# Planning the first eight expert tiles early and running the end of the first attention among them

## What is computed

```python
h = _L0_tok_ref(x, L0_tok_W, L0_tok_b)             # moving averages, then a projection
h = h + _L0_attn_ref(_layernorm(h, axis=-1), ...)  # causal softmax attention, 16 heads
h = h + _L0_ffn_ref(_layernorm(h, axis=-1), ...)   # 8 experts, 256 -> 1024 -> 256, top 2 a token
h = h + _L1_attn_ref(h, ...)                       # sigmoid(s) * exp(s) attention
h = h + _L1_ffn_ref(_layernorm(h, axis=-1), ...)   # fp8 product
```

## Time and profile before

| | us |
|---|---|
| median of 3 runs | 851.28 (846.99 to 853.36) |
| the profiled execution | 855.8 |
| its span, first to last instruction | 854.0 |
| TensorE busy | 730.1 (85%), mean granted clock 0.911 |
| first attention | to about 264 |
| tiles, from the first second layer | 308.9 to 591.4 |
| second attention | 591 to about 817 |
| fp8 layer | to 854 |

### The profile page before, as it was taken

One profiled execution on the slowest core, in us unless ns is written; L12 is line 12 of the kernel. 1 busy time (PEld: TensorE's weight loads), 2 busy tenths in 40 slices (PEclk: granted clock), 3 DMA queues, 4 the chain that ended last, 5 costly groups with the idle time before them and its releaser, 6 DMA issues. The chain is left out here.

```text
span 854.0 us, 15973 instructions
## 1 busy us (share of the span) xinstructions
PE 730.1 (85%) x5604; PEld 580.3 (68%) x5604; DVE 447.0 (52%) x1111; ACT 349.9 (41%) x596; POOL 121.7 (14%) x166
## 2 busy tenths in 40 slices
PE   6488989889886299999999999998589888898646
PEld 5367767767664199999999999997366555664312
DVE  4536776776465222333223132231667888766677
ACT  3143345325432022222222132223687888988513
POOL 2010131232123300000010000101332223100000
PEclk9799999999999599999999999999798988998855
DMA  7989366346541555555565559740764466642002
GB/s 178 206 127 211 45 84 81 64 65 87 72 114 52 177 206 198 179 181 172 173 202 185 182 152 230 218 173 31 112 90 65 66 79 100 74 54 23 1 13 86
DMA packets 70710, 102.66 MB, mean 120 GB/s; under 512 B 8160, under 2 KB 58472, under 8 KB 70512
## 3 DMA queue, kind: packets, MB, share of 16 engines
q1 hardware_dynamic: 66928, 92.82, 49.0%
q0 software_dynamic: 3136, 8.40, 3.3%
q10 hardware_dynamic: 576, 0.52, 0.2%
HBM read 63.88 MB, written 12.58 MB: 90 GB/s over the span
## 5 line engine op out<-in xcount | busy, mean ns | idle before, releaser
L1623 PEld LDWEIGHTS psum<-arena 128*128 128x128 f32 x1248 | 147.1, 194 | 3.5 <-issue 1.7
L1623 PE MATMUL psum<-arena 128*128 128x128 f32 x1248 | 147.7, 277 | 1.1 <-ACT arena L1254 1.1
L1657 PE MATMUL psum<-arena 128*128 x624 | 141.3, 379 | 1.2 <-DVE arena L1458 1.2
L1657 PEld LDWEIGHTS psum<-arena 128*128 128x128 f32 x624 | 115.5, 190 | 15.7 <-issue 1.6
L1248 ACT ACTIVATE arena<-psum,arena 128x128 f32<-128x128 f32 x156 | 44.5, 368 | 197.4 <-PE psum L1623 140.3
L1585 PE MATMUL psum<-arena 96*128 96x256 bf16 x512 | 84.4, 299 | 26.3 <-ACT arena L1219 15.1
L1451 DVE TENSOR_SCALAR arena<-psum,arena 128x128 f32<-128x128 f32 x156 | 43.9, 344 | 94.7 <-PE psum L1623 75.2
L1585 PEld LDWEIGHTS psum<-arena 96*128 96x128 bf16 x512 | 47.1, 103 | 62.3 <-ACT arena L1219 26.9
L1343 DVE TENSOR_TENSOR arena<-arena 128x1024 f32<-128x1024 f32 x64 | 80.0, 1314 | 5.5 <-ACT arena L1218 3.1
L1219 ACT ACTIVATE arena<-psum,neg_mu 128x1024 f32<-128x1024 f32 x64 | 68.9, 1118 | 13.8 <-PE psum L1585 8.2
L1188 POOL DMA_INDIRECT w0T<-yg,pos x32 | 31.1, 971 | 301.0 <-DMA yg<-arena 239.3
(11 more groups left out here) (248 smaller groups left out, 1157.9 us busy)
## 6 DMA issues: line engine op xcount, KB each, us to landing
arena<-in_L_ffn_w_dram SPq DMA_DIRECT2D x47, 1024.0 KB, 5.4
arena<-arena SPq DMA_DIRECT2D x192, 128.0 KB, 6.0
arena<-xg SPq DMA_DIRECT2D x39, 128.0 KB, 2.0
yg<-arena SPq DMA_DIRECT2D x39, 128.0 KB, 1.7
out_dram<-arena SPq DMA_DIRECT2D x8, 256.0 KB, 2.1
arena<-in_x_dram SPq DMA_DIRECT2D x8, 128.0 KB, 7.3
arena<-in_L_ffn_b_dram SPq DMA_DIRECT2D x1, 1024.0 KB, 12.2
xg<-zeros SPq DMA_DIRECT2D x5, 128.0 KB
```

Source lines behind the costliest of these rows:

```text
L1623: mm = pe.matmul(psum[:, 2 * v + c // HALF, (c % HALF) * P:(c % HALF + 1) * P], w1b[:, i % W1_BUFS, d, c * P:(c + 1) * P], xtT[:, v, d, :] ...
L1657: mm = pe.matmul(y_bank, hidT[:, u, c, :], w2s[:, one(e), c, :].rearrange("p o n -> p (o n)"), start=(c == 0), stop=(c == HC - 1))
```

## The change

Blocks 1 and 2 become one. All engines but GpSimd stop `batches` after iteration 7. What iterations 8 and 9 did is written out as `drain_...` pieces and set among the steps of the first tiles, from step -2 to step 3.

The list of tiles is made in two parts. From the counts after five batches (`EARLY_BATCHES`) DVE picks tiles that are full already (`early_valid` at the end of iteration 6, `early_grid` and `early_list` in iteration 7, with two products of TensorE each), and lists the first eight. SP loads the weights and rows of tile 0 as soon as that list is there and the rows of five batches have landed. The rest of the list (`late_valid`, `late_grid`, `late_list`) is made in steps 3 and 4; from tile 8 on SP waits for it, for all scatters, and for the zero rows, which SP now writes alone, all eight in its step 4.

A tile list in two parts makes the slots harder to find: 22 small DVE steps in place of ten, in steps 11 to 14. `gather(0)` waits for 24 tiles in place of 16, and so everything for the first batch stands seven steps later; `combine(1)`, `stat1(1)` and `norm1(1)` stand two later, in steps 36, 37 and 38. Some banks of PSUM change places. Iteration 0 to 5 of the first attention, the work of a tile, the second attention and the fp8 layer are as before.

```diff
+EARLY_TILES, EARLY_BATCHES = 8, 5
...
-        def batches(eng, iteration):
+        def batches(eng, iteration, end):
 
             for b in range(-2, 2):
                 iteration(b, b % 2, b // 2)
             with eng.Fori(0, (B - 4) // 2) as it:
                 for u in range(2):
                     iteration(it * 2 + (2 + u), u, it + 1)
-            for b in range(B - 2, B + 2):
+            for b in range(B - 2, end):
                 iteration(b, b % 2, b // 2)
...
-                batches(sp, iteration)
-
+                batches(sp, iteration, B)
...
                 load_w2(7)
-                zero_tails(sp, range(0, EXPERTS, 2))
-                sp.wait_ge(S["p_step"], TILE_E_STEP)
+                sp.wait_ge(S["st_mm"], PAIRS * (B - 1))
+                sp.wait_ge(S["p_step"], EARLY_STEPS)
                 load_w1(sp, 0)
-                sp.wait_ge(S["zfill"], 16 * (EXPERTS + 1))
                 for u in range(2):
-                    sp.wait_ge(scat[u], 16 + 16 * TOPK * QT * B // 2)
-                sp.wait_ge(S["p_step"], PLAN_STEPS)
+                    sp.wait_ge(scat[u], 16 + 16 * TOPK * QT * ((EARLY_BATCHES + 1 - u) // 2))
                 load_tile(sp, 0)
-
+                sp.wait_ge(S["st_mm"], PAIRS * B)
+
...
+                def tile(i, u):
+                    if i == 2:
+                        sp.dma_start(w8, a["L1_ffn_weight"].rearrange("(j p) i -> p j i", p=P)).then_inc(S["w8_in"], 16)
+                    if i + 3 == EARLY_TILES:
+                        sp.wait_ge(S["p_step"], PLAN_STEPS)
+                        sp.wait_ge(S["zfill"], 16 * (EXPERTS + 1))
+                        for s in range(2):
+                            sp.wait_ge(scat[s], 16 + 16 * TOPK * QT * B // 2)
+                    if has(i + 3) and i + 3 >= 1:
+                        wait(sp, S["tx_mm"], i + 2)
+                        load_tile(sp, i + 3)
+                        wait(sp, S["l1_hi"], i + 4 - W1_BUFS)
+                        load_w1(sp, i + 3)
+                    if i == 4:
+                        zero_tails(sp, range(EXPERTS))
+                    if has(i):
+                        sp.wait_ge(S["y_ev"], i + 1)
+                        sp.dma_start(yg[i * P:(i + 1) * P, :], yt[:, u]).then_inc(y_st[u], 16)
...
+                    done = min(EARLY_TILES + 2 * EXPERTS, MOE_TILES) if b == 0 else min(2 * EXPERTS * (b + 1), MOE_TILES)
+                    pool.wait_ge(S["place_step"], PLACE_STEPS)
+                    for u in range(2):
+                        pool.wait_ge(y_st[u], 16 * ((done + 1 - u) // 2))
...
+                batches(act, iteration, B)
...
+                    if i == 0:
+                        drain_back()
+                    if i == 2:
+                        drain_input(7)
                     if has(i + 2):
                         act.wait_ge(S["tx_mm"], i + 3)
                         wait(act, S["l1_hi"], i + 1)
                         act.copy(xtT[:, u].rearrange("p c t -> p (c t)"), x_bank).then_inc(S["xtT_done"], 1)
+                    if i == -2:
+                        drain_input(6)
...
+                def early_valid():
+
+                    plan(dve.scalar_tensor_tensor(out=valid[:], in0=run[:], scalar=cand_full[:, 0:1], in1=cand_sel[:],
+                                                  op0=ALU.is_gt, op1=ALU.mult))
+                    assert plan_steps[0] == EARLY_VALID
+
+                def early_grid():
+
+                    dve.wait_ge(S["plan_mm"], 1)
+                    plan(dve.tensor_reduce(place[:], early_place, AX, ALU.add))
+                    plan(dve.tensor_scalar(early_flag[:], place[:], float(EARLY_TILES), None, ALU.is_le))
+                    plan(dve.tensor_scalar(passed[:, 0:EARLY_TILES], iota_t[:, 0:EARLY_TILES], place[:, 0:1], None, ALU.is_ge))
+                    plan(dve.tensor_scalar(chosen[:], valid[:], early_flag[:, 0:1], None, ALU.mult))
+                    assert plan_steps[0] == EARLY_GRID
+
+                def early_list():
+
+                    dve.wait_ge(S["plan_mm"], 2)
+                    listed(early_cand, 0, EARLY_TILES)
+                    plan(dve.tensor_copy(chosen_of[:], early_kept))
+                    assert plan_steps[0] == EARLY_READ
+                    rows_of(0, EARLY_TILES)
+                    assert plan_steps[0] == EARLY_STEPS
+
+                def late_valid():
+
+                    plan(dve.tensor_copy(cnt[:], run[0:1, :]))
+                    plan(dve.scalar_tensor_tensor(out=valid[:], in0=run[:], scalar=cand_min[:, 0:1], in1=cand_sel[:],
+                                                  op0=ALU.is_gt, op1=ALU.mult))
+                    plan(dve.tensor_tensor(left[:], valid[:], chosen[:], ALU.subtract))
+                    assert plan_steps[0] == VALID_STEP
+
+                def late_grid():
+
+                    dve.wait_ge(S["plan_mm"], 3)
+                    plan(dve.tensor_reduce(place[:], plan_place, AX, ALU.add))
+                    plan(dve.tensor_tensor(tiles_of[:], plan_tiles, chosen_of[:], ALU.add))
+                    n = MOE_TILES - EARLY_TILES
+                    plan(dve.tensor_scalar(passed[:, 0:n], iota_t[:, 0:n], place[:, 0:1], None, ALU.is_ge))
+                    assert plan_steps[0] == GRID_STEP
+
+                def late_list():
+
+                    dve.wait_ge(S["plan_mm"], 4)
+                    listed(plan_cand, EARLY_TILES, MOE_TILES)
+                    rows_of(EARLY_TILES, MOE_TILES)
+                    assert plan_steps[0] == PLAN_STEPS
...
+                    if isinstance(b, int) and b == EARLY_BATCHES + 2:
+                        early_grid()
...
+                    if isinstance(b, int) and b == EARLY_BATCHES + 2:
+                        early_list()
...
+                    if isinstance(b, int) and b == EARLY_BATCHES + 1:
+                        early_valid()
+
+                batches(dve, iteration, B)
...
+                    if i == -1:
+                        drain_turned()
+                        gate_logits(6, misc[0])
+                    if i == 0:
+                        choose_experts(6)
+                    if i == 1:
+                        drain_sum()
+                    if i == 3:
+                        choose_experts(7)
+                    if i == 4:
+                        late_grid()
                     if has(i):
                         e = expert_of(i)
                         dve.wait_ge(S["l2_mm"], i + 1)
                         wait(dve, y_st[u], 16 * (i // 2))
                         dve.tensor_tensor(yt[:, u], y_bank, b2r[:, one(e), :].rearrange("p o d -> p (o d)"),
                                           ALU.add).then_inc(S["y_ev"], 1)
+                    if i == 1:
+                        drain_norm()
+                        rank_tokens(6, 0, dispatched(B // 2, 0, -3))
+                    if i == 2:
+                        gate_logits(7, misc[0])
                     if i == 3:
+                        rank_tokens(7, 1, dispatched(B // 2, 1, -3))
+                        late_valid()
+                    if i == 4:
+                        late_list()
+                    if i == 11:
+                        dve.memset(n_vaug[:, :, :, :, DH:32], 1.0).then_inc(S["set_done"], 1)
+                        dve.memset(amax[:, 1], 0.0).then_inc(S["set_done"], 1)
                         split_slots()
-                    if i == 4:
+                    if i == 12:
+                        slot_levels()
+                    if i == 13:
+                        slot_counts()
+                    if i == 14:
                         tile_slots()
-                    if i == 19:
+                    if i == 26:
                         combine(0)
-                    if i == 20:
+                    if i == 27:
                         stat1(0)
-                    if i == 21:
+                    if i == 28:
                         norm1(0)
-                    if i == 25:
+                    if i == 32:
                         split_rest(0, 0, S["n_qh"], S["n_qr"])
-                    if i == 26:
+                    if i == 33:
                         split_rest(0, 1, S["n_kh"], S["n_kr"])
                         split_last(0, 0, S["n_qm"], S["n_ql"])
-                    if i == 27:
+                    if i == 34:
                         split_last(0, 1, S["n_km"], S["n_kl"])
-                    if i == 28:
+                    if i == 35:
                         biased_v(0, 0)
-                    if i == 34:
+                    if i == 36:
                         combine(1)
-                    if i == 35:
+                    if i == 37:
                         stat1(1)
-                    if i == 36:
+                    if i == 38:
                         norm1(1)
...
+                    if isinstance(b, int) and b == EARLY_BATCHES + 2:
+                        pe.wait_ge(S["p_step"], EARLY_VALID)
```

(98 more changed lines are left out.)

890 lines of the change are left out of this document (452 added, 438 removed).

## The result

The changed kernel takes 824.48 us (median of 4 runs, 821.51 to 827.78) against 849.87 us (4 runs, 846.99 to 853.36): a ratio of 0.970, 95% interval 0.9644 to 0.9757. The forecast was 824.3 us, range 818 to 833.

What follows compares the result with a forecast made beforehand. TensorE bounds the tiles; ahead of them one chain from batch 7's output projection to tile 0's load leaves a hole. Gain 28.8 - 0.4 (iteration 7) - 1.4 (hand-over) = 27.0 us, off 851.28: 824.3 us, range 818 to 833.

Steps and rivals of the forecast that it cites:

- The hole: From the first attention's last product to tile 4's second layer: TensorE's waiting ahead of the tiles goes, gain 28.8 us.
- the drained pieces: Remaining steps of the first attention set among tiles 0 to 4: 6.8 us of TensorE's work, none waiting.
- loss of the block's border is already in the 28.8: Border between blocks 1 and 2: VectorE's 6.47 us idle there counted within the 28.8 us gain ahead of the tiles.
- it does not do what it says: Rival: first tile still waits for something late, only the border is saved, 3 to 5 us: 847 us; chance 0.04.
- The head stalls: Rival, first five tiles: slacks beside the softmax chain add up wrong, 5 to 10 us lost, 829 to 834; chance 0.18.
- The low-clock case: Rival "slower", in the tiles: interleaved small pieces keep TensorE's clock at half, 882 us at eight tiles; chance 0.03.
- The gate: SP's new wait ahead of tile 8: slack 1.7 us, cost zero, bounds 0 to 3; late-gate rival 825 to 828, chance 0.13.
- Iteration 7: First attention's iteration 7: added early-list steps on DVE and small TensorE products lose 0.4 us, bounds 0.2 and 1.5.
- The hand-over: Tiles to second attention: `norm1(1)`, now in step 38, delays `turned_input(1)`; 1.4 us lost, bounds 0 and 2.
- hand-over hidden: Rival: the later normalisation costs nothing, late gate and head clean, 822.5 us; chance 0.62 together with the forecast as worked out.
- The second attention longer than before by more than 1.4 us, of which nothing here speaks: Last listed sign, in the profile after, that the prediction is wrong; no term of the forecast covers it.
- The range's lower end: 818 us, from hand-over 1.4, iteration 7 0.2, small products priced high 0.5, and as much again for a run's surroundings.

## Why the prediction came out

**The hole: right, for a reason half mistaken.** The list of terms held. With the last product at 260.1 and not 264.2, tile 4's second layer was to end at 308.4 and ended at 307.5: first layer at 1.5 us behind the product as forecast, no wait, and 45.9 us of work from 261.64 to 307.53 rather than 46.8. By the distances between starts the tiles took 40.4 of them (40.0 forecast) and the drained pieces 5.5 (6.8): the gate logits 1.6 for 2.06, the output projection 1.7 for 1.99, ranks and plan products 0.4 for 0.9. That is the 0.9 by which 28.8 was short. But "loss of the block's border is already in the 28.8", with VectorE's 6.47 us idle as its measure, named a cause that was none: with that border alone gone, tile 4 came not a tenth of a microsecond sooner. VectorE stood at the border while TensorE stood for the rows of tile 0, and only the second is on the path. The rival "it does not do what it says" carried the same mistake: 3 to 5 us saved by the border alone would have been some 3 us lost (2.8 at the end; 0.4% in the ratio).

**The head stalls: it did not.** The slacks that were costed at nothing held; TensorE waits nowhere from 261.64 to 307.5. The low-clock case did not come either: 1.00 throughout.

**The gate: no stall, with less in hand.** Slack 1.1 us where the sum had 1.7. The loads were not late: with everything 4.1 us earlier, the rows of tile 8 were to be issued at 315.4 and were at 315.47 (a zero row cost 1.12 where 1.07 was taken, but the load came 2.2 behind the last of them and not 2.5). TensorE came to them earlier than forecast, at 318.46 and not 319.3, by the 0.9 that the pieces ahead were cheaper. The Trainium skill (Perfetto Trace Analysis, DMA Instruction — HWDGE (DVE, Sync)) warns of a surprisingly long delay of the semaphore behind a write to HBM. The trace shows none that goes with the target: of 128 KB each, the stores to HBM landed after 1.7 us and the zero rows after 2.7, the rows loaded from HBM after 2.0; the gate held.

**Iteration 7: within the bounds, wrong in kind.** 0.4 was forecast, with 0.2 to 1.5 as bounds; the last two iterations show 0.8 on average (52.9 against 52.1), double the forecast. But the instructions that were added up cost nothing to be seen. VectorE's flags and list lie in idle time:

```profile
235.13 0.22 DVE L1057 SCALAR_TENSOR_TENSOR valid<-run,cand_full,cand_sel 128x8 bf16<-128x8 f32 x1
236.00 7.01 DVE L1110 TENSOR_REDUCE arena<-psum 128x6 f32<-128x768 f32 x8 [0.65 <-PE psum L1579]
...
249.91 0.15 DVE L1045 TENSOR_SCALAR tile<-psum 1x8 f32<-1x8 f32 x1 [3.38 <-PE psum L1696]
```

The flags end at 235.35 and the maxima wait 0.65 more for TensorE's scores; from the start of the norm ahead of them (L971, L690 before) to the end of the eight maxima both kernels take 8.5 us. What differs is the granted clock. Iteration 7, from copy to copy of the attention's output, takes 24.6 to 24.8 us in the three profiles of the old order, with a clock of 0.73 to 0.75 in the three microseconds from 13.65 us on. The changed order's nine profiles have 0.76 or 0.77 there twice, with 24.5 and 24.6 us: nothing lost. Five have 0.50, with 25.7 to 26.2: a microsecond or more. (The last two, 0.60 and 0.64, follow a longer iteration 6, and the two together took 53.1 and 53.3.) Whether the added steps bring the clock back later, or the nine profiles only fell so, was not tried and stays open.

**The hand-over: right.** 1.4 forecast, 1.5 seen in the first pair and 1.5 given back by the run that moves the normalisation. The rival "hand-over hidden" falls; its 822.5 should have been 822.9, the 824.3 less 1.4.

**The end: missed.** "The second attention longer than before by more than 1.4 us, of which nothing here speaks" is what happened, by 2.7 us, at its far side. The prediction followed what the merge does to the border it removes and not to the one it leaves. Its scatters had been drained at the removed one; now GpSimd drains 64 indirect DMAs at the next, 2.8 us longer. The drain ran in the trace of before, twice, on its block lines. The Trainium skill (Runtime: NRT & Kernel Launch, Instruction fetch mechanics) is cited in the prediction for the stall of a taken branch at a border; the runs show 0.3 us for all at this border that is not the drain.

**The sum** was right within 0.2 us by luck in part. By the measured terms: -29.7 - 0.2 + 0.8 + 1.5 + 2.7 = -24.9, against -25.4 between the medians. The missed 2.7 makes the gain smaller, the 0.9 of the small pieces makes it larger, and the kernel before's median came out 1.4 lower with its fourth run (849.87, not 851.28); together they nearly cancel. In the medians of the first four runs each none of the small terms can be seen; only the stretches show them. The range's lower end does not follow from its own terms either: 1.4, 0.2 and 0.5, and as much again, give 820.1 and not 818. The result lies within both.

## What to carry to other kernels

An engine's idle time at a block's border is not the border's price: look which engine's wait is on the path, and take the border away alone to see. When blocks are merged, follow what each engine still owes at the border that is left; software DMAs of GpSimd are paid for at its next drain, and a drain placed in its idle time, or no border behind it, makes that free. A hole that one chain sets has two remedies, to start the next work without the chain and to run it beside the chain; here each was worth half. The second alone was not run; a tile can't start without an entry in the list, so it needs the first.

## What was not expected of the hardware

- GpSimd's DRAIN takes 0.08 to 0.09 us for each software DMA since the drain before it (0.817 us at none, 3.431 at 32, 6.227 at 64 or, with its two first DMAs, 66, each with the 0.70 us power ahead of it), though the last gather was issued at 675.5, some 100 us before it.
- A DMA of zeros to rows read from a register and one to rows known beforehand took 13.8 / 8 = 1.72 us of SP's queue together (1.66 in the last pairs), where the first kind alone takes 1.12 each. Whether the register or the other target makes the difference was not tried.
- Without a change to them, the hand-over came out 1.7 us longer with a granted clock of 0.84 than with 1.00 in its first 11 us (24.8 against 23.1 us), and the stretch behind the last product 1.7 to 2.2 us longer with 0.82 to 0.67 than with 0.97. What decides which of them a run gets is not shown.
